# Cross-attention and mixture of experts on one core: the routing of each group moved one batch ahead, second ranks before the last values, two weight splits on GpSimd

## The reference

```python
x = x + xattn(layernorm(x), ctx, ctx, mask, gamma, beta)     # softmax(q k^T / 16, masked) @ v, then layernorm * gamma + beta
x = x + ffn(layernorm(x), w_gate, w_gate_up, w_down)

def ffn(x, w_gate, w_gate_up, w_down):                       # 8 experts, 2 per row, F = 1024
    gate_probs = softmax(x @ w_gate)
    topk_vals, topk_idx = top_k(gate_probs, 2)               # kept, scaled to a sum of 1
    g, u = split(einsum('bsd,edh->ebsh', x, w_gate_up))
    expert_out = einsum('ebsf,efd->ebsd', silu(g) * u, w_down)
    return einsum('bse,ebsd->bsd', gate_probs, expert_out)
```

## Time and profile before

| | |
|---|---|
| median of 3 runs | 433.06 us (432.96 to 433.12) |
| the profiled execution | 433.62 us |
| its span, first to last instruction | 431.2 us |
| TensorE busy | 420.3 us (97%) |
| VectorE busy | 303.7 us (70%) |
| ScalarE busy | 215.7 us (50%) |
| GpSimd busy | 196.0 us (45%) |

### The profile page before, as it was taken

How to read it: one execution, slowest core, us unless ns; L and a number is a source line. 1 busy time by engine, 2 the same in 40 slices (tenths; PEclk the granted TensorE clock), 3 DMA queues, 4 the chain that set the end, 5 groups by cost and what they waited for, 6 DMA issues and landing times.

```text
span 431.2 us, 10111 instructions
## 1 busy us (share of the span) xinstructions
PE 420.3 (97%) x2340; PEld 350.1 (81%) x2340; DVE 303.7 (70%) x749; ACT 215.7 (50%) x461; POOL 196.0 (45%) x217
## 2 busy tenths in 40 slices
PE   9999799999999999999999999999999999999995
PEld 6887467888888888888888888888888888888885
DVE  4779988886885678768765568758776568865633
ACT  4886726546554455455633365546544356434431
POOL 6444253564544345644544444445554344444312
PEclk9999999999999999999999999999999999999999
DMA  8778324543454135515531125533552234112212
GB/s 213 215 237 261 126 75 144 152 135 68 131 147 111 26 86 160 132 32 152 151 75 26 25 38 130 165 87 76 146 148 36 39 71 126 27 25 31 33 14 24
DMA packets 28620, 44.16 MB, mean 102 GB/s; under 512 B 2833, under 2 KB 22219, under 8 KB 28587
## 3 DMA queue, kind: packets, MB, share of 16 engines
q1 hardware_dynamic: 20358, 32.96, 25.0%
q0 software_dynamic: 7520, 10.41, 14.3%
q10 hardware_dynamic: 709, 0.32, 0.3%
HBM read 34.04 MB, written 9.65 MB: 101 GB/s over the span
## 4 chain that ended last, share of the span: by engine, by line
PE 88%; DVE 4%; DMA 3%; ACT 2%; SPq 1%; issue 1%; POOL 0%; DVEq 0%; POOLq 0%
PE bank L1462 48%; PE bank L1485 16%; PE bank L1487 8%; PE bank L1475 8%; PE bank L1446 2%; DMA vals<-in_ctx 2%; PE bank L1335 1%; PE bank L1325 1%; DMA tok<-rows_d,gather_i 1%; PE bank L1302 1%; PE bank L1257 1%; PE bank L1532 1%; ACT ctxT L1116 1%; DVE x_sb L706 1%; SPq L428 1%
## 5 line engine op out<-in xcount | busy, mean ns | idle before, releaser
L1462 PE MATMUL bank<-w,tokT_hi 128*128 (+1 forms) x616 | 169.4, 397 | 1.0 <-DVE tokT_lo L927 0.9
L1179 ACT ACTIVATE gated<-bank,row_rstd 128x512 f32<-128x512 f32 x77 | 53.0, 688 | 172.4 <-PE bank L1462 172.4
L1462 PEld LDWEIGHTS bank<-w,tokT_hi 128*128 128x128 f32 x616 | 110.0, 188 | 22.6 <-DVE tokT_lo L927 1.2
L1485 PE MATMUL bank<-w,aT_hi 128*128 (+1 forms) x304 | 116.4, 417 | 0.2 <-DVE w L402 0.2
L936 DVE SCALAR_TENSOR_TENSOR act<-bank,row_rstd,gated 128x512 f32<-128x512 f32 x77 | 57.6, 748 | 77.6 <-ACT gated L1179 77.2
L592 POOL DMA_INDIRECT out<-y_sb,out_i x39 | 62.1, 1592 | 86.3 <-DVE y_sb L957 83.0
L1462 PE MATMUL bank<-w,tokT_lo 128*128 (+1 forms) x308 | 95.4, 391 | 0.0
L1487 PE MATMUL bank<-w,aT_lo 128*128 (+1 forms) x304 | 85.2, 280 | 0.0
L579 POOL TENSOR_TENSOR tok<-tok,beta_b 128x256 f32<-128x256 f32 x36 | 26.2, 728 | 99.5 <-DMA tok<-rows_d,gather_i 99.5
L1462 PEld LDWEIGHTS bank<-w,tokT_lo 128*128 128x128 f32 x308 | 57.8, 188 | 12.6
L1485 PEld LDWEIGHTS bank<-w,aT_hi 128*128 128x128 f32 x304 | 57.2, 188 | 10.5 <-DVE w L402 0.4
(11 more groups left out here) (190 smaller groups left out, 409.9 us busy)
## 6 DMA issues: line engine op xcount, KB each, us to landing
raw<-in_L_ffn_w_gate_up SPq DMA_DIRECT2D x32, 512.0 KB, 3.8
raw<-in_L_ffn_w_down SPq DMA_DIRECT2D x16, 512.0 KB, 3.8
rows_d<-x_sb SPq DMA_DIRECT2D x8, 265.0 KB, 4.7
x_sb<-in_x SPq DMA_DIRECT2D x8, 256.0 KB, 7.5
out<-x_sb SPq DMA_DIRECT2D x8, 256.0 KB, 4.6
out<-y_sb,out_i POOLq DMA_INDIRECT x39, 3.8
tok<-rows_d,gather_i POOLq DMA_INDIRECT x38, 3.8
cap<-in_mask_BxSxS_ik SPq DMA_DIRECT2D x1, 462.0 KB, 6.1
```

The source lines that it names most:

```text
L1179: act_e.activation(gated[:, h, :], ps_g[h][:, :], ACT.Silu, scale=row_rstd[:, s:s + 1]).then_inc(gated_set, 1)
L1462: ins = pe.matmul(ps[:, :], tokens_[:, s, k, :], w.rearrange("p a g d -> p (a g) d"), start=(k == 0 and tokens_ is tokT_hi and part == 0), ...
L1485: pe.matmul(ps_y[:, :], aT_hi[:, h, c, :], w.rearrange("p a t d -> p (a t d)"), start=(h == 0 and c == 0), stop=False, skip_group_check=True)
```

## The change

On VectorE `choose` of the first group moves from step 4 to step 3, its `slots` from 5 to 4, its `places` and `select` from 6 to 5; `choose` of the second group stands alone in step 6, and its `places` move into step 7, ahead of the last `x1`. `split_low` of piece 0 stays in step 4, of piece 1 moves to step 6, and of pieces 2 and 3 go to GpSimd, behind its last `scales`. In the last group the product by the row number is done by VectorE for two tiles and by ScalarE for the two tiles of `FAR`, and the first four steps of the block tables stand between the steps of `slots`. TensorE does the first ranks in step 4 and the second ones ahead of the last `values`. ScalarE copies the turned context ahead of two `centre`, and rounds piece 3 behind the loop. SyncE loads pieces 3, 4 and 5 later. GpSimd issues the gather of block 2 before `row_scale(1)`. The first products of block 0 wait for the high part of the rows alone.

```diff
+    FAR = GROUPS[-1][len(GROUPS[-1]) // 2:]
...
-                if 1 <= b < 1 + PIECES - RAW:
-                    load_piece(0, RAW + b - 1)
+                if b == 4:
+                    load_piece(0, RAW)
+                if b == 6:
+                    load_piece(0, RAW + 1)
+            load_piece(0, PIECES - 1)
...
                 scales(i - 1)
                 if i + 1 < B:
                     values_gamma(i + 1)
+            split_low(pool, 2)
+            split_low(pool, 3)
...
             split_table()
+            gather(2, gather_i[:, 2:3])
             row_scale(1)
-            gather(2, gather_i[:, 2:3])
...
+                last = i == len(GROUPS) - 1
                 dve.tensor_tensor(slot_c[:, part, :], ps_rank[:, part, :], chosen[:, part, :], ALU.mult).then_inc(rank_read, 1)
+                if last:
+                    step(tables, dve.tensor_scalar(count_up[:], ps_count, float(P - 1), None, ALU.add))
...
+            def select_last(i, g):
+
+                near, far = g[:len(g) // 2], g[len(g) // 2:]
+                dve.wait_ge(lo_set, i + 1)
+                part = halved(place_of_group[i][:, 0:columns(near), :])
+                dve.tensor_tensor(part, part, over_slots(number_4, near), ALU.mult).then_inc(last_place, 1)
+                match(token_of_group[i][:, 0:columns(near), :], near, neg_hi).then_inc(token_set, 1)
+                match(token_of_group[i][:, columns(near):columns(g), :], far, neg_hi).then_inc(token_set, 1)
...
-                if i == 4:
-                    split_low(dve, 0)
-                if i == 5:
-                    split_low(dve, 1)
                 if i + 1 < B:
                     masked_logits(i + 1)
                 x1(i - 1)
-                if i == 4:
+                if i == 3:
                     dve.wait_ge(const, 15)
                     choose(GROUPS[0])
+                if i == 4:
+                    slots(0, GROUPS[0])
+                    split_low(dve, 0)
                 if i == 5:
-                    slots(0, GROUPS[0])
-                    split_low(dve, 2)
-                if i == 6:
                     places(0, GROUPS[0])
                     select(0, GROUPS[0])
+                if i == 6:
                     choose(GROUPS[1])
+                    split_low(dve, 1)
                 if i == 7:
                     slots(1, GROUPS[1])
+                    places(1, GROUPS[1])
             choose(GROUPS[2])
-            places(1, GROUPS[1])
             select(1, GROUPS[1])
             slots(2, GROUPS[2])
             places(2, GROUPS[2])
-            select(2, GROUPS[2])
+            select_last(2, GROUPS[2])
...
             tok_low(0, 0)
             row_gate(0, 0, 0)
-            split_low(dve, 3)
...
+                if i in CTX_AT:
+                    copy_ctxT(CTX_AT[i])
                 if i == 2:
                     centre(6)
                     centre(7)
-                if i in CTX_AT:
-                    copy_ctxT(CTX_AT[i])
                 if 3 <= i < 6:
                     split_high(act_e, i - 3)
-                if i == 7:
-                    split_high(act_e, 3)
+            split_high(act_e, 3)
             numbers(0, GROUPS[0])
-            numbers(1, GROUPS[1])
             split_high(act_e, 4)
             act_e.activation(silu_ready[:], neg_half[:, 0:1], ACT.Silu)
+            numbers(1, GROUPS[1])
+            numbers(2, FAR)
             split_high(act_e, 5)
...
-                values(i - 1)
                 if i == B:
                     ranks(1, GROUPS[1])
+                values(i - 1)
...
-                if i == 5:
+                if i == 4:
                     ranks(0, GROUPS[0])
...
                 if h == 0:
+                    pe.wait_ge(tokT_hi_set, b + 1)
+                if h == 0 and later(b, 1):
                     pe.wait_ge(tokT_lo_set, b + 1)
...
                     for tokens_, part in ((tokT_hi, 0), (tokT_hi, 1), (tokT_lo, 0)):
+                        if not later(b, 1) and h == 0 and tokens_ is tokT_lo:
+                            pe.wait_ge(tokT_lo_set, b + 1)
```

More of the change, by code:

```diff
@@ L744, in slots @@
                 step(route, dve.tensor_reduce(both[:, part], slot_c[:, part, :], X, ALU.add))
+                if last:
+                    after(tables)
+                    step(tables, dve.tensor_scalar(blocks_i[:], count_up[:], P.bit_length() - 1, None, ALU.arith_shift_right))
                 after(route)
                 step(route, dve.tensor_tensor(slot[:, part, 0], both[:, part], slot[:, part, 1], ALU.subtract))
+                if last:
+                    after(tables)
+                    step(tables, dve.tensor_scalar(padded[:], blocks_i[:], float(P), float(P), ALU.mult, ALU.max))
                 after(route)
                 step(route, dve.tensor_scalar(hi[:, part, :], slot[:, part, :], 0.5 - P / 2, ROUND, ALU.add, ALU.add))
+                if last:
+                    after(tables)
+                    step(tables, dve.tensor_tensor(cum_part[:], up_to[:], padded[:].unsqueeze(1).to_broadcast([P, E, E]), ALU.mult))
                 after(route)
@@ L764, in select @@
             def select(i, g):
-                if i == len(GROUPS) - 1:
-                    dve.wait_ge(lo_set, i + 1)
-                    dve.tensor_tensor(halved(place_of_group[i]), halved(place_of_group[i]), over_slots(number_4, g), ALU.mult).then_inc(last_place, 1)
                 match(token_of_group[i], g, neg_hi).then_inc(token_set, 1)
+            def select_last(i, g):
[5 more added lines that the diff above has]
+                match(token_of_group[i][:, columns(near):columns(g), :], far, neg_hi).then_inc(token_set, 1)
             def row_centre(b, s):
@@ L827, in block_columns @@
                 after(tables)
-                step(tables, dve.tensor_scalar(jump[:], padded[:], -1.0 / P, float(FULL), ALU.mult, ALU.add))
                 step(tables, dve.tensor_tensor(past[:], block_start[:].unsqueeze(2).to_broadcast([P, NBLK, E - 1]), per_block(ends, P), ALU.is_ge))
@@ L895, in _ @@
             places(2, GROUPS[2])
-            select(2, GROUPS[2])
-            step(tables, dve.tensor_scalar(count_up[:], ps_count, float(P - 1), None, ALU.add))
+            select_last(2, GROUPS[2])
             after(tables)
[L900 to L904, removed]
+            step(tables, dve.tensor_reduce(ends[:], cum_part[:], X, ALU.add))
+            step(tables, dve.tensor_scalar(jump[:], padded[:], -1.0 / P, float(FULL), ALU.mult, ALU.add))
             dve.wait_ge(token_ps, len(GROUPS))
@@ L908, in _ @@
             dve.tensor_tensor(gather_0[:], ps_token[:, 0:1], spare_0[:], ALU.add).then_inc(gather_0_set, 1)
-            after(tables)
-            step(tables, dve.tensor_reduce(ends[:], cum_part[:], X, ALU.add))
-            after(tables)
             block_columns()
@@ L1358, in tokens @@
                 for t in g:
+                    if t == FAR[0]:
+                        pe.wait_ge(token_set, i + 2)
+                    if t in FAR:
+                        pe.wait_ge(place_set, GROUPS[-1][0] + t - FAR[0] + 1)
                     if i < len(GROUPS) - 1:
```

## The result

| | before | changed |
|---|---|---|
| median of 3 runs | 433.06 us | 437.68 us (437.41 to 437.92) |
| ratio, 95% interval | | 1.0107 (1.0088 to 1.0126) |
| profiled execution | 433.62 us | 437.92 us |
| its span | 431.2 us | 436.2 us |
| TensorE busy | 420.3 us | 422.2 us |

The forecast was 433.9 us, at most 435.3.

The account below looks back on a forecast made before the run. VectorE and what it feeds bound 42 to 58 us, TensorE 70 to 424 us. Items 2 to 7 summed to +1.05 us, with part of item 1 +0.9, on 433.06: about 433.9 us, range 431.9 to 435.3.

Parts of the forecast that it names:

- Item 1: Loop, ScalarE and TensorE: context copy no longer waits behind two `centre`, first ranks take most back; about 0 to -0.3 us.
- item 2: VectorE up to the last `x1`: `x1` of batch 5 about 0.75 us earlier, the last `x1` 0.3 us earlier.
- 7: gather of block 2: Gather no longer waits for `row_scale(1)`: TensorE's wait goes, -0.4 us, and sequencer catch-up, -0.2 us.
- main mechanism: Shared port: GpSimd's two splits hold VectorE's steps with SBUF inputs until they end; main case, chance 0.48, 433.2 to 434.8 us.
- items 5 and 6: Address to first rows, -0.2 us; first products not waiting for the low part, -0.45, and piece 3 split earlier, -0.3.
- item 4: From `chosen` to the address: less VectorE work, 4.6 us instead of 5.6, -1.0 us.
- Item 3: GpSimd's two splits hold `versus` and its successor: last `chosen` at 50.3 instead of 46.67 us, +3.6 us.
- this case's own range: The main case's range, 433.2 to 434.8 us, where GpSimd's splits hold VectorE.
- item 5: Address to first rows: `ends` and `jump` done earlier, then the gather limits; 3.4 us instead of 3.6, -0.2 us.
- Item 8: Loads: pieces 3 and 4 touch ScalarE only while ahead of VectorE; TensorE waited for no later piece; 0 us.
- first rival: GpSimd's splits do not hold VectorE, ScalarE bounds before the address; -0.95 us, 432.1 us, chance 0.30.
- rival of a worse order: GpSimd's first split precedes the match of `places(1)`, or the second follows directly; 1 to 2 us more, 435.3 us, chance 0.13.

Follow-up runs that it names:

- spin18: The changed kernel with 18 spin products instead of 3 behind the wait for the last `x1`; 434.0 us, ratio 1.0022 to the kernel before.
- before_pool: The kernel before with only the splits of pieces 2 and 3 moved to GpSimd behind its last scales; ratio 1.0141 to the kernel before.
- on_vector: The changed kernel with the splits of pieces 1, 2 and 3 on VectorE, none on GpSimd; 434.1 us, ratio 1.0024 to the kernel before.
- vector_spin_act: `vector_spin` with ScalarE's second `numbers` ahead of the rounding of piece 4 and the table load; ratio 0.9992 to the kernel before.
- vector_spin: `on_vector` with the spins around the wait for the last `x1` raised from 3 + 3 to 9 + 6; ratio 1.0046 to the kernel before.

## Why the prediction was wrong

Item 1, -0.15 us in the forecast, and the 0.75 us that item 2 gives to `x1` of batch 5 can't be told from how the loop differs between executions (36.51 to 38.76 us against 37.77 before).

The direction was right and the size was not: I put +0.9 us, it is +4.6, outside the range. By its own steps, shifts of the profiled executions:

| step | predicted | measured |
|---|---|---|
| 2, 3: to the last `chosen`, with GpSimd's splits | +3.6 | +3.05 |
| 4: from `chosen` to the address, VectorE's work | -1.0 | -1.12 (spin18) |
| 4: the same, TensorE at its lower clock | not in the sum | +2.70 |
| 5, 6: address to the second half of block 0 | -0.95 | -0.05 |
| 7: gather of block 2 | -0.6 | -0.54 |
| sum, up to `down` of block 1 | +1.05 | +4.04 |

**The main mechanism held.** Which engine has the port was walked correctly: one split under `x1`, `versus` behind it, the second split between `versus` and its successor. A split on GpSimd that hardly had to wait took 2.34 us (4.67 for two in `before_pool`) where I put 2.45. The hold itself was forecast a little too long: from the last `x1` to the end of `chosen` 6.4 us, measured 5.73, before 2.46, because `versus` and `cap` end 0.3 us behind the split that holds them and do not start afresh there. With the clock held (`spin18`) the whole change costs +1.0 us (0.1 to 1.8). That this is close to the sum is in part luck: two errors, 0.55 us too much here and 0.9 too much gain in items 5 and 6, cancel for the most part.

**The step that failed is item 4.** It went from `chosen` to the address along VectorE alone, and took TensorE's part as following its data. My reading of the stretch from 42 to 58 us called TensorE's work there "much of it `spin`" and went on; I did not ask what these products are for. Item 3 said that `chosen` comes 3.6 us later and left open what TensorE does in that time. The answer was in the trace of the kernel before: TensorE has three fillers there, 0.82 us at 45.15, so it must idle for most of the time that VectorE is held. No row of before showed a wait of this length, so its price was unknown and should have been bounded: between nothing and the stretch to the address at the lower clock, 32 products of `tokens` and ten fillers. At the full clock they take 0.07 us (0.83 for twelve) and 0.22 us each (0.81 for three, with an overlap), as much again at half of it: 32 x 0.07 + 10 x 0.22 = 4.4 us as the most, of which 2.7 came. The whole bound on top of this case's own range would have reached 439.2 us and taken in the 437.68 measured; half of it, 437.0, would not.

**Items 5 and 6 counted limits one by one that stand side by side.** Taking 0.45 us from the first products was right for these products (1.92 to 1.45 us behind the first `centre`) and worthless for the end. The split of piece 3 was no gain either: with it on VectorE (`on_vector`, before) the second half starts 5.11 us behind the first `centre`, without it 5.02. Before, VectorE's register loads ran behind that split, and it idled 0.55 us for them; in the changed kernel it idles 1.32 us, and its `centre` of block 1 comes 4.28 us behind the first instead of 4.33. TensorE then waits for it. Of item 5 nothing came, 3.64 us instead of 3.59: the two small steps done early freed VectorE, but it waits 0.37 us for the gather.

**Item 8 was right for this kernel only.** TensorE waited for no weights here, and ScalarE's 1.09 us for piece 4 passed while VectorE was held. Once the hold was gone, ScalarE's 1.35 us for piece 4 stood in front of the `numbers` that set the address (`on_vector`), and then its wait for piece 5 in front of the table (`vector_spin_act`).

The first rival (the splits don't hold VectorE) is out: `versus` and `cap` were held alike, to within 0.03 us, in four executions. It was a near thing: GpSimd's first split was issued at 43.23 us, a tenth behind VectorE's `match` at 43.12. The rival of a worse order did not come in the change, but in `before_pool`.

What stays open: how much of the 0.9 us that accrue behind `down` of block 1 belongs to the change, and why the clock comes back at different times.

## What to carry to other kernels

A wait on one engine has a second price on TensorE: ask how long TensorE has nothing to do meanwhile, and what is queued behind the wait that would then run at half the clock. Filler products are sized for the gaps of one schedule; whoever moves a wait must size them again, and check that they don't stand on the chain when the clock is lost. Long elementwise steps go to GpSimd only where VectorE does nothing over SBUF that anyone waits for, a tiny step included.

## What the runs showed of the hardware

- GpSimd's split of 128x1024 held VectorE's steps over SBUF to its own end or 0.3 us beyond, whatever their size: 24 columns took 2.21 us, 256 took 1.65 and 2.45. The trace agrees with the Trainium skill (SBUF — State Buffer, Who interferes with whom), by which the shared port pair is an exclusive lock for the whole instruction and a `tensor_scalar` can use it too. `x1`, with its other input in PSUM, was not held (0.88 us).
- With 4.1 us of idle TensorE the granted clock was 0.52 from 48.5 to 55 us. Behind gaps of 1.56 and 0.85 us (`on_vector`) and behind 0.26, 0.21 and 0.70 us with 0.5 in pieces (`vector_spin`) it fell as well, while the kernel before, with 0.53, 0.85 and 0.56 us, kept it, and so did `spin18` with 1.42 and 0.90 us around 4.06 us of work. So the longest gap alone doesn't tell. The Trainium skill (TensorE: Matmul & The Clock Gate, Part 1) has two levels, the lower one for an idle engine; the trace agrees on the levels (1.00 and 0.50), and in the changed kernel on the idle engine.
- The fall shows up late: in the changed kernel TensorE idled from 45.76 us on, the granted clock was 1.00 up to 48.5 and 0.50 from 49 to 55. It is what comes behind the gap that pays.
